# Attention inside a macaron block: weighted values taken two steps at a time, with four probability buffers and four score banks

## The reference

```python
x = L0_attn_x
x = x + 0.5 * _L0_ffn_ref(_layernorm(x, axis=-1), ...)   # attention, then a mixture of experts
x = x + _L0_attn_ref(_layernorm(x, axis=-1), ...)        # attention alone
x = x + 0.5 * _L0_ffn_ref(_layernorm(x, axis=-1), ...)
# in each of them:
scores = jnp.einsum('bqhd,bkhd->bhqk', q, k) / jnp.sqrt(jnp.float32(HD))
scores = jnp.where(causal[None, None], scores, jnp.finfo(scores.dtype).min)
attn = jax.nn.softmax(scores, axis=-1)
ao = jnp.einsum('bhqk,bkhd->bqhd', attn, v)
```

## Time and profile before

| | |
|---|---|
| runs before | 2004.94, 2005.07, 2009.96 us; median 2005.07 |
| profiled execution, its own time | 2009.72 us |
| its span, first to last instruction | 2008.0 us |
| PE busy | 1725.7 us, 86% |
| DVE busy | 1379.9 us, 69% |
| ACT busy | 1072.2 us, 53% |
| mean granted clock of PE | 0.903 |
| score matmuls (L843), first and last start, over the three passes | 82.9 and 1796.9 us |

### The profile page before, as it was taken

One profiled execution on the slowest core, in us unless ns is written; L12 is line 12 of the kernel. 1 busy time (PEld: TensorE's weight loads), 2 busy tenths in 40 slices (PEclk: granted clock), 3 DMA queues, 4 the chain that ended last, 5 costly groups with the idle time before them and its releaser, 6 DMA issues. The chain is left out here.

```text
span 2008.0 us, 30183 instructions
## 1 busy us (share of the span) xinstructions
PE 1725.7 (86%) x10630; PEld 741.5 (37%) x10630; DVE 1379.9 (69%) x2728; ACT 1072.2 (53%) x2289; POOL 427.6 (21%) x483
## 2 busy tenths in 40 slices
PE   3799999999759936899999998469999999975994
PEld 1233333333247723333333332233333333324673
DVE  5789999986243347888989881378899998715234
ACT  1255677677614412446766768124577767761441
POOL 4500101111015626100101020250011110100662
PEclk9789999999859967889999999677999999995997
DMA  3420203200011134200202000242011020000112
GB/s 98 109 49 2 46 6 98 63 2 1 1 29 39 43 102 133 49 1 2 49 2 49 2 1 2 65 124 49 2 25 26 2 49 2 2 1 21 40 43 76
DMA packets 59096, 75.47 MB, mean 38 GB/s; under 512 B 9319, under 2 KB 51884, under 8 KB 57640
## 3 DMA queue, kind: packets, MB, share of 16 engines
q1 hardware_dynamic: 50680, 57.77, 11.5%
q0 software_dynamic: 4992, 9.32, 1.7%
q10 hardware_dynamic: 3264, 6.29, 1.0%
HBM read 52.84 MB, written 21.43 MB: 37 GB/s over the span
## 5 line engine op out<-in xcount | busy, mean ns | idle before, releaser
L734 ACT ACTIVATE probs<-ps 128x512 f32<-128x512 f32 (+3 forms) x1920 | 885.2, 541 | 500.1 <-PE ps L843 497.8
L585 DVE TENSOR_REDUCE mpart<-ps 128x1 f32<-128x512 f32 (+3 forms) x1680 | 1017.8, 665 | 119.5 <-PE ps L797 75.2
L797 PE MATMUL ps<-ka,qa 96*128 96x512 bf16 (+3 forms) x1920 | 669.3, 370 | 40.6 <-DVE ps L566 28.6
L843 PE MATMUL ps<-qa,ka 96*128 96x512 bf16 (+3 forms) x1920 | 632.3, 357 | 24.5 <-ACT probs L734 22.2
L856 PE MATMUL ps<-probs,vv 128*9 128x512 f32 (+3 forms) x3840 | 443.1, 534 | 1.8 <-POOL probs L683 1.8
L683 POOL TENSOR_SCALAR_AFFINE_SELECT probs<-probs 128x512 f32<-128x512 f32 x192 | 121.9, 635 | 1213.0 <-ACT probs L734 1213.0
L797 PEld LDWEIGHTS ps<-ka,qa 96*128 96x128 bf16 x1920 | 191.8, 100 | 470.6 <-DVE mpart L585 322.4
L843 PEld LDWEIGHTS ps<-qa,ka 96*128 96x128 bf16 x1920 | 183.5, 99 | 259.4 <-ACT probs L734 144.9
L800 PE MATMUL ps<-mask_rows,identb 128*128 128x128 bf16 x768 | 159.9, 233 | 0.0
L1153 DVE SCALAR_TENSOR_TENSOR probs<-probs,slot_w,ps 128x448 f32<-128x448 f32 x78 | 53.0, 680 | 124.3 <-PE ps L1094 124.3
L856 PEld LDWEIGHTS ps<-probs,vv 128*9 128x9 f32 x3840 | 57.1, 88 | 142.4 <-ACT probs L734 97.3
(11 more groups left out here) (159 smaller groups left out, 1097.2 us busy)
## 6 DMA issues: line engine op xcount, KB each, us to landing
qa<-qsplit SPq DMA_DIRECT2D x27, 384.0 KB
ka<-ksplit SPq DMA_DIRECT2D x27, 384.0 KB
probs<-rope ACTq DMA_DIRECT2D x12, 512.0 KB, 8.1
arena<-results SPq DMA_DIRECT2D x16, 256.0 KB, 4.8
qsplit<-arena SPq DMA_DIRECT2D x9, 384.0 KB, 4.1
ksplit<-arena SPq DMA_DIRECT2D x9, 384.0 KB, 2.6
qa<-qsplit SPq DMA_DIRECT2D x36, 96.0 KB
ka<-ksplit SPq DMA_DIRECT2D x36, 96.0 KB
```

What stands on the lines that cost most here:

```text
L585: dve.tensor_reduce(mpart[:, j % MD, h0:h0 + some, qt, kc], ps[:, bank, 0:some * w].rearrange("p (h w) -> p h w", h=some), axis=AX.X, op=A ...
L734: act.activation(probs[:, s % 2, h, 0:n], ps[:, u % SB, 0:n], ACT.Exp, scale=SCALE).then_inc(probs_ready, 1)
L797: ins = pe.matmul(dst, qa[0:KROWS, b, h0 + k, tile * 128:(tile + 1) * 128], ka[0:KROWS, b, h0 + k, kc * CH:kc * CH + n], start=True, stop= ...
L843: pe.matmul(dst, ka[0:KROWS, b, h, kt * 128:(kt + 1) * 128], qa[0:KROWS, b, h, c * CH + q0:(c + 1) * CH], start=True, stop=True).then_inc( ...
```

## The change

`SB` goes from 3 to 4 score banks, so the fillers move to banks 4 to 6, and the value sums share one bank, 7, in place of two; the first values of a chunk therefore wait for the evacuation of the chunk before, not of the one before that. Two more probability buffers lie in `arena`, which the first stage of a pass uses for the split operands, so ACT waits once per pass, at step 2, for the last stores from it. In the planner the values of two steps are issued together, behind the scores of an odd step s: those of steps s-3 and s-2. Its assumed time for a value group is now 4 x n / 2.4 ns plus 200 for the first of a pair and 20 for the second, where it was plus 60 for each. The line that places fillers (`main`, which calls `fill`) is as before, and is called for each of the two value groups.

```diff
-SB, MB = 3, 3
+SB, MB = 4, 3
+VS, PD = 2, 4
...
-    for s in range(len(steps) + 1):
+    for s in range(len(steps) + VS):
...
-                act = max(act, pe + hop, values_at.get(s - 2, 0.0) + hop) + 52 + n * 0.83
+                act = max(act, pe + hop, values_at.get(s - PD, 0.0) + hop) + 52 + n * 0.83
...
-        if s:
-            pj, pk = steps[s - 1]
-            n = CH - max(0, pk - TPC * chunks[pj][1]) * 128
-            masking = 900 if pk >= TPC * chunks[pj][1] else 0
-            main(exp_at[HPG * s - 1] + hop + masking, 4 * n / 2.4 + 60, min(j, len(chunks) - 1))
-            values_at[s - 1] = pe
-            events.append(("values", s - 1, pj, pk))
...
+        if s % VS == VS - 1:
+
+            for v in range(max(0, s - 2 * VS + 1), s - VS + 1):
+                pj, pk = steps[v]
+                n = CH - max(0, pk - TPC * chunks[pj][1]) * 128
+                masking = 900 if pk >= TPC * chunks[pj][1] else 0
+                main(exp_at[HPG * v + HPG - 1] + hop + masking, 4 * n / 2.4 + (200 if v % VS == 0 else 20),
+                     min(j, len(chunks) - 1))
+                values_at[v] = pe
+                events.append(("values", v, pj, pk))
...
+    pring = [probs[:, 0, :, :], probs[:, 1, :, :], third, fourth]
...
-                        if s >= 2 and h == 0:
-                            act.wait_ge(values_weighted, s - 1)
+                        if s >= PD and h == 0:
+                            act.wait_ge(values_weighted, s - PD + 1)
+                        if s == 2 and h == 0:
+                            act.wait_ge(part2_ready, 2 * NC)
+                            for i in range(2 * NC - PB, 2 * NC):
+                                act.wait_ge(parts_stored[i % PB], stored(i))
...
-                        if kt == 0 and j >= 2:
-                            pe.wait_ge(output_copied, j - 1)
+                        if kt == 0 and j >= 1:
+                            pe.wait_ge(output_copied, j)
```

## The result

The changed kernel takes 2043.48 us (median of 4 runs, 2037.93 to 2047.62), the kernel before 2005.79 (4 runs); the ratio is 1.018 with a 95% interval from 1.015 to 1.021. It is slower by 38 us. The prediction was 2028, with a range from 2008 to 2048: sign and range hold.

What follows compares the result with a forecast made beforehand. PE was taken to bound chunks 4 to 13, and a loop of waits between PE and ACT chunk 15. Terms of -3.8, +1.3, +3, +5.2 and +2 gave +7.7 us per pass, +23.1 for three: 2028.2 us, range 2008 to 2048.

Steps and rivals of the forecast that it cites:

- Pairing, 0: Value groups: 71 of 80 pairs have another instruction between them, so both groups pay the full 0.20 us; saving 0.
- Rival A: Value-group pairs: pairing pays despite a row maximum between, 14.2 us less per pass, 1985.6 us in all; chance 4%.
- End of the core, -3.8: Last steps: row maxima fill six more steps (-3.0), eight pairs run slightly shorter (-0.8); -3.8 us per pass.
- The loop of the pairs: Ending of the core: two steps run as a pair take 4.77 us against 4.87 before.
- Full stretch, +1.3: Chunks 4 to 13: pairs' last scores wait for banks, +1.3 us per pass; at most 1.8 us could be won.
- Runs ahead of chunks 1 to 3, +3: Row-maximum runs at DVE's pace: 12 row maxima move in from between scores; +3 us per pass.
- Wait at chunk 15, +5.2: First score of chunk 15 waits for the DMA chain behind its maxout, formerly hidden; +5.2 us per pass.
- PE's clock behind it, +2: After the idle at chunk 15 PE's granted clock falls to half for some 5.7 us; +2 us per pass.
- The rest: 0: ACT's wait at step 2, the one value bank, and DMAs the same in number and size cost nothing; 0.
- the third: Sign in the trace: PE as full in chunks 4 to 13, and these chunks within a few us of 243.
- the sixth: Sign in the trace: first score of the pass to first score of chunk 3 longer by about 3 us.

Runs made afterwards that it cites:

- e1: Changed kernel with SP's order alone put back: six operand loads issued behind the next guard store and load; 2011.34 us, ratio to before 1.003.
- e5: Changed kernel with each pair's second value group directly behind the first, and row maxima placed up to 200 ns early; 2021.91 us, ratio 1.0083.
- e9: Kernel of e5 with DVE reducing only the first half of each row maximum's columns and a sixteenth of the scale; 1914.49 us (one execution).
- e7: Kernel of e1 with 23 extra matmuls of 512 columns filling PE's idle ahead of chunk 15's first score; 2014.74 us, ratio 1.0039.
- e6: Changed kernel without pairs: four score banks kept, values one step at a time, one step behind, 60 ns planned per value group; 1976.86 us, ratio 0.9845.
- e8: Kernel of e1 with DVE reducing only the first half of each row maximum's columns and a sixteenth of the scale; 1978.76 us (one execution).
- e3: Changed kernel with e1's SP order, and row maxima placed up to 400 ns early once chunk 13 runs; 2015.53 us, ratio 1.0054.
- e12: Kernel of e3 with the halved reductions and small scale of e8; 1968.29 us (one execution).
- e10: Kernel of e6 with SP alone changed: six operand loads issued ahead of the guard store of chunks 6 and 10; 2011.73 us, ratio 1.0022.
- e13: Changed kernel with the six operand loads issued by ACT on its own queue, behind the exponentials of steps 44 and 84; 2039.23 us, ratio 1.0163.

## Why the prediction came out as it did

*The sum was +7.7 per pass, the core's growth is 11.2.* Without the missed mechanism it is 2.2 (e1), 2.8 with the value groups behind the last exponential. The median lies in the range because a term that was missing (9.0) is larger than what the others were too high (about 5): the number is luck. Pairing, the wait and the clock behind it were read rightly.

*Pairing, 0: right.* Both groups pay in full. Rival A falls with it. That 0.20 is the price of standing alone, read off two widths of one line, agrees with e5 (1.84 for two) and e9 (9.3 us for 46 pairs).

*End of the core, -3.8: right in sum, less so in its parts.* By step 132, 19 row maxima more are open than before; at 0.22 they would lengthen chunk 14 by 4.2 us. Without its idle it is 2.0 longer (37.2 - 4.9 - 30.3): 2.2 went into empty places. That is less than the 3.0 forecast. Chunk 15 at full clock (e7) takes 36.6 for 38.3, 1.7 less, of which 0.6 is paid back behind its last exponential: 1.1, more than the 0.8 forecast. Together -3.3. The loop of the pairs was forecast at 4.77 us, and takes 4.76 (1811.13 to 1815.89):

```profile
1811.13 3.00 PE L855 MATMUL ps<-qa,ka 96*128 96x512 bf16 x8
1814.06 1.90 PE L868 MATMUL ps<-probs,vv 128*9 128x512 f32 x16
1815.89 3.00 PE L855 MATMUL ps<-qa,ka 96*128 96x512 bf16 x8
```

*Full stretch, +1.3: a little high.* Chunks 3 to 13 of e1 are 4.5 us shorter than before, of which the 19 row maxima that left are 4.2: on balance nothing was lost to the lag or the banks. The bound of 1.8 us that could be won does not hold. In e6 chunks 4 to 13 are 5.0 us shorter than before, with only 0.6 us less of row-max matmuls; where two scores follow each other, before loses 3.0 us in pass 0, from start to start against 0.21 for 512 columns, e6 loses 0.2, and only 1.3 of the 3.0 shows as idle. A stretch that looks full can still have waits in it.

*Runs ahead of chunks 1 to 3, +3: mis-sized.* Chunks 0 to 2 grew by 0.4. The runs did grow, from 29.8 to 39.2 us, from the last score of a chunk to the first of the next. But the time between the scores shrank by 9.0, from 66.0 to 57.0: each of the 12 row maxima gave back 0.75 there, where the step took 0.22 or 0.42 as its price. Why it is so much stays open. Halving the reductions takes 8.3 us off the runs and 1.7 off the time between scores (e8), so with the new order DVE sets the pace in the runs and hardly between the scores; the share of the half clock was not separated.

*Wait at chunk 15, +5.2: right as an idle (4.9), and not to be had back as simply as it sounds.* Pulling the row maxima forward removed it and gained nothing (e3), where DVE was busy 9.25 of 10 us ahead of it; with shorter reductions it gave 4.9 (e12).

*PE's clock behind it, +2: right in kind, somewhat high.* 1.0 to 1.6 us in the changed kernel by comparison with e7, within its bounds of 0 and 4.

*"The rest: 0": the step that failed.* It says that DMAs are the same in number and size, and the step on the wait adds that the next tightest maxouts, of chunks 7 and 11, have 7 us of cover for a chain of 5.3. Both are true, and the wrong question. The chain's length was taken from places where no other DMA ran, and the order was read on PE alone. The maxouts of chunks 6 and 10 slipped by 3 and 6 steps past the reload, whose place does not move, and with that the store went behind 2.3 MB: 14.7 us in place of 2.7. The prediction did name more traffic as a reason for a longer chain, but only at chunk 15. Price: 9.0 us per pass, more than every other term. Of the points that were to show the prediction wrong, the third (chunks 4 to 13 within a few us of 243) is the one that caught it; the sixth (3 us more up to chunk 3) failed as well, with 0.4.

## What to carry to other kernels

When a planner's costs change, read the new order on every queue: a wait and a bulk transfer that swap places on SP can cost more than all that moves on PE. Price a chain of DMAs with the traffic that will stand ahead of it. And take a change apart before dropping it: here one of its parts (a fourth score bank for the second accumulator, values one step behind) is 1.5% faster than the kernel before, while the part that names the change pays only where the engine that empties the other banks has room.

## What the runs showed of the hardware

At this place a 12 KB store lands in 1.4 us (e1) or 2.7 (before) with nothing ahead of it, in 14.7 (after) and 15.1 (e10) behind six loads of 384 KB on the same queue, and in 12.3 (e13) on another queue while those loads run. The DMA engines in after, in 40 slices of 0.65 us from 230 to 256 (busy tenths; the mean share from 236.5 to 251.2 is 0.66, not the 0.9 of the expectation of e13):

```profile
DMA  0100000909959495949393949393912000000000
```

Why a store on a queue of its own still takes 12.3 us was not shown.

An idle of PE of 2.08 us behind dense work was followed by a fall of the granted clock (0.64 over 4.8 us, which is 3.5 us at half). Length alone does not tell: in pass 1 of after, 1.75 us of idle ahead of chunk 10 was followed by such a fall, and 1.75 us ahead of chunk 6 was not. First chunk 6, then chunk 10, from the first score on:

```profile
990.46:995.26 4.80, 4.80 (x38) 2.15 (x39) 4.04 (x7) 4.18 (x9) 0.00 (x0) 1.00 0.01 2
1098.08:1102.88 4.80, 4.80 (x14) 2.02 (x15) 2.77 (x4) 2.86 (x5) 0.00 (x0) 0.50 0.00 0
```

How long the low stretch lasts was not settled by what PE did: behind the same idle of 4.9 us, with the same instructions, e1 has 7.2 us at 0.50 in pass 0, and in pass 1 a mean of 0.79 over the first 8.13 us, 3.4 us at half:

```profile
1221.87:1230.00 8.13, 7.97 (x48) 2.77 (x48) 1.24 (x3) 7.65 (x16) 0.00 (x0) 0.79 0.00 0
```

And a busy PE can be waiting: its modelled durations (0.38 us for a matmul that costs 0.22) hide waits of up to 0.16 us each, some 15 us in chunks 4 to 13 of e5, while the windows show PE as full:

```profile
272.00:312.00 40.00, 39.83 (x284) 14.78 (x284) 33.41 (x67) 26.68 (x58) 2.54 (x4) 1.00 0.04 6
```
